# The last batch's output stages of a Mamba and SwiGLU block as a program of their own, with the last quad weighed in two parts

## The reference

```python
h  = x * rsqrt(mean(x*x) + 1e-5) * norm_w
xs, res = split(h @ in_proj_w.T)                  # 256 + 256 channels
u  = silu(conv4(xs) + conv_b)
delta, Bm, Cm = split(u @ x_proj_w.T, [64, 80])   # 64 + 16 + 16
delta = softplus(delta @ dt_proj_w.T + dt_proj_b)
state[t] = exp(delta * A) * state[t-1] + delta * u * Bm     # 256 channels x 16 states
y  = (sum over 16 states of state * Cm) + u * D
a  = (y * silu(res)) @ out_proj_w.T + x
x1 = layernorm(x + a)
out = layernorm(x1 + (silu(x1 @ wg.T) * (x1 @ wu.T)) @ wd.T)   # 384 hidden; weights are integers / 127
```

## Time and profile before

| | us |
|---|---|
| median of 3 runs | 580.98 |
| lowest, highest | 580.44, 583.85 |
| the profiled execution | 581.86 |
| its span, first to last instruction | 580.1 |

### The profile page before, as it was taken

One profiled execution on the slowest core, in us unless ns is written; L12 is line 12 of the kernel. 1 busy time (PEld: TensorE's weight loads), 2 busy tenths in 40 slices (PEclk: granted clock), 3 DMA queues, 4 the chain that ended last, 5 costly groups with the idle time before them and its releaser, 6 DMA issues.

```text
span 580.1 us, 6345 instructions
## 1 busy us (share of the span) xinstructions
PE 476.2 (82%) x1887; PEld 239.6 (41%) x1887; DVE 521.0 (90%) x562; ACT 367.2 (63%) x581; POOL 417.0 (72%) x214
## 2 busy tenths in 40 slices
PE   8988774989979996989978996989888996587574
PEld 6332431535542553534442553444443452243243
DVE  5869789998999899998999899999999899999924
ACT  3577865489458866589458866589458855544220
POOL 8758597857695796968695796868695796876010
PEclk9889976989979898989979897989979997769879
DMA  8063333600642032600551042501451042500000
GB/s 222 3 146 62 83 72 74 145 1 5 141 108 56 1 82 67 160 1 15 131 120 46 0 97 62 149 0 24 121 131 31 0 101 70 138 1 0 1 18 18
DMA packets 27368, 39.22 MB, mean 68 GB/s; under 512 B 3816, under 2 KB 10056, under 8 KB 27344
## 3 DMA queue, kind: packets, MB, share of 16 engines
q1 hardware_dynamic: 25424, 38.51, 27.9%
q10 hardware_dynamic: 1920, 0.42, 0.4%
HBM read 3.27 MB, written 2.10 MB: 9 GB/s over the span
## 4 chain that ended last, share of the span: by engine, by line
PE 27%; issue 23%; DVE 21%; POOL 18%; ACT 6%; DMA 2%; SPq 1%; POOLq 0%; DVEq 0%; ACTq 0%
DVE state L1038 14%; POOL prod L864 10%; PE dense_ps L464 6%; PE dense_ps L482 5%; PE y_ps L456 4%; DVE weighted L1046 3%; POOL z_wm L868 2%; ACT decay_ps L620 2%; POOL z_wm L870 2%; PE c_ps L442 1%; PE dense_ps L484 1%; PE dense_ps L506 1%; POOL z_wm L881 1%; PE dense_ps L502 1%; SPq L358 1%
## 5 line engine op out<-in xcount | busy, mean ns | idle before, releaser
L864 POOL TENSOR_TENSOR prod<-du_rep,b_rep 128x2048 f32<-128x2048 f32 x63 | 285.6, 4540 | 52.0 <-ACT b_rep L657 32.8
L1038 DVE TENSOR_TENSOR_SCAN state<-decay_ps,prod 128x512 f32<-128x512 f32 x256 | 299.1, 1207 | 19.5 <-ACT decay_ps L620 13.4
L620 ACT ACTIVATE decay_ps<-delta_rep,a_neg 128x512 f32<-128x512 f32 x252 | 170.6, 688 | 107.3 <-DVE state L1038 107.1
L1046 DVE TENSOR_TENSOR weighted<-state,c_ps 128x2048 f32<-128x2048 f32 x64 | 146.4, 2288 | 4.2 <-PE c_ps L442 2.3
L464 PE MATMUL dense_ps<-x_all,ident 128*128 128x256 f32 x348 | 102.5, 430 | 18.9 <-ACT bc L653 9.4
L464 PEld LDWEIGHTS dense_ps<-x_all,ident 128*128 128x128 f32 x348 | 67.1, 207 | 65.9 <-issue 21.2
L456 PE MATMUL y_ps<-weighted,gather 128*32 128x512 f32 x512 | 77.7, 683 | 17.0 <-DVE weighted L1046 17.0
L482 PE MATMUL dense_ps<-h_t,tap_t 128*128 128x512 f32 x128 | 58.5, 599 | 0.9 <-ACT h_t L668 0.9
L442 PE MATMUL c_ps<-bc,pick 64*128 64x512 f32 x64 | 34.7, 542 | 19.7 <-DVE weighted L1046 19.7
L442 PEld LDWEIGHTS c_ps<-bc,pick 64*128 64x128 f32 x64 | 12.8, 200 | 69.6 <-issue 38.5
L889 POOL TENSOR_TENSOR ve<-mv,epsm 128x4 f32<-128x4 f32 x14 | 2.8, 202 | 53.1 <-DVE mv L1057 53.1
(11 more groups left out here) (148 smaller groups left out, 628.6 us busy)
## 6 DMA issues: line engine op xcount, KB each, us to landing
du_rep<-z_wm SPq DMA_DIRECT2D x64, 256.0 KB, 4.7
delta_rep<-z_ln SPq DMA_DIRECT2D x64, 256.0 KB, 4.5
out_dram<-y_out SPq DMA_DIRECT2D x8, 256.0 KB, 2.2
state<-L_attn_in_proj_w_in ACTq DMA_DIRECT2D x1, 256.0 KB, 3.9
x_all<-L_attn_x_in SPq DMA_DIRECT2D x1, 256.0 KB, 4.3
weighted<-L_ffn_w_gate_in SPq DMA_DIRECT2D x1, 192.0 KB, 9.8
weighted<-L_ffn_w_up_in SPq DMA_DIRECT2D x1, 192.0 KB, 3.5
weighted<-L_ffn_w_down_in SPq DMA_DIRECT2D x1, 192.0 KB, 4.5
```

Source lines behind the costliest of these rows:

```text
L620: A(decay_ps[n % DECAYS][:, :], decay_ps[n % DECAYS][:, :] if spread_first else delta_rep[:, h, c, :], ACT.Exp, scale=a_neg[:, col:col + 1 ...
L864: TT(prod[quad % 2][:, :, :], du_rep[:, h, :, :], b, ALU.mult).then_inc(prod_ready, 1)
L1038: dve.tensor_tensor_scan(state[n // BLOCKS % 2][:, n % BLOCKS, :], decay_ps[n % DECAYS][:, :], prod[n // BLOCKS % 2][:, n % BLOCKS, :], 0. ...
L1046: TT(weighted[quad % 2][:, :, :], state[quad % 2][:, :, :], c_ps[:, :].unsqueeze(1).broadcast_to([P, BLOCKS, T]), ALU.mult).then_inc(weigh ...
```

## The change

Iteration 8 becomes a function `tail` of its own on PE, DVE and ACT, with semaphores of its own (`last_...`), and POOL's two powers are called there directly. In it:

- **The last quad is weighed in two parts.** In iteration 7, DVE weighs blocks 0 to 2 (1536 columns) before the last scan and block 3 (512 columns) after it. PE sums blocks 0 to 2 after the first part and block 3 after the second.
- **`proj` starts early.** Twice x and the part of g's half 0 are issued ahead of the last quad's sum; only the part of half 1 follows it.
- **Two half banks.** The 512 rows are split into two halves of two row blocks, in dense banks 0 and 1 (`half_ps`). Statistics start on a half when its bank is done. The scaling of half 0 is DVE's, that of half 1 ACT's (with a shift `nmr` = -mean * rs that DVE computes first); the transposes, and the copies to `x1_t`, are done by halves on the two engines.
- **All eight banks.** The six gate and up products go to six different banks (`rest_ps`), in the order gate0, up0, gate1, up1, gate2, up2, with no wait for a bank; `down(0)` stands ahead of up2. The x1 term of `down` is issued ahead of gate0.
- **Silu.** ACT applies Silu to the gate's bank, DVE multiplies with up in one instruction. The Silu table is asked for ahead of time by an activation of one column.
- **The store** is two transfers of 128 KB, SP's for half 0 and ACT's for half 1.

In the jobs of all batches, `proj` and `down` now go through their terms in the outer loop and the row blocks in the inner one, and wait for each term's input apart.

```diff
@@ PE: jobs of all batches
-                    it.wait(pe, g_ready, HALVES, -1, HALVES)
-                    for i in range(TILES):
-                        for h in range(HALVES):
+                    for h in range(HALVES):
+                        it.wait(pe, g_ready, HALVES, -1, h + 1)
+                        for i in range(TILES):
                             last = mm(ps[:, i * P:(i + 1) * P], g[:, h, i * P:(i + 1) * P], out_t[:, h, :],
...
-                    it.wait_taken(pe, f"up{HID - 1}")
-                    for i in range(TILES):
-                        for b in range(HID):
+                    for b in range(HID):
+                        it.wait_taken(pe, f"up{b}")
+                        for i in range(TILES):
@@ banks
+        half_ps = dense_ps[0:2]
+        rest_ps = decay_ps + dense_ps[2:] + [c_ps, y_ps]
@@ PE, iteration 8
+            def tail(it):
+                for b in range(DENSE):
+                    pe.wait_ge(taken[b], it.before[b])
+                pe.wait_ge(g_ready, HALVES * B - 1)
+                for half in range(2):
+                    for i, cols in half_tiles(half):
+                        mm(half_ps[half][:, cols], twice[:, :], x_all[:, (B - 1) * TILES + i, :],
+                           start=(cols.start == 0), stop=False)
+                        mm(half_ps[half][:, cols], g[:, 0, i * P:(i + 1) * P], out_t[:, 0, :], start=False, stop=False)
+                for c in range(BLOCKS):
+                    if c == 0:
+                        pe.wait_ge(last_weighed, 1)
+                    if c == BLOCKS - 1:
+                        pe.wait_ge(last_weighed, 2)
+                    last = mm(y_ps[DB * c:DB * c + DB, :], gather[:, :], weighted[(QUADS - 1) % 2][:, c, :],
+                              start=False, stop=True, tile_position=(0, DB * c))
+                last.then_inc(last_summed, 1)
+                pe.wait_ge(g_ready, HALVES * B)
+                for half in range(2):
+                    for i, cols in half_tiles(half):
+                        last = mm(half_ps[half][:, cols], g[:, 1, i * P:(i + 1) * P], out_t[:, 1, :],
+                                  start=False, stop=(i % HT == HT - 1))
+                    last.then_inc(last_full, 1)
...
+                for half in range(2):
+                    pe.wait_ge(last_x1[half], 1)
+                    for i, cols in half_tiles(half):
+                        last = turn(rest_ps[half][:, cols], x1[:, i, :], ident[:, :])
+                    last.then_inc(last_turned, 1)
+                for half in range(2):
+                    for i, cols in half_tiles(half):
+                        mm(half_ps[half][:, cols], ident[:, :], x1[:, i, :], start=(cols.start == 0), stop=False)
...
+                gate_or_up(gate_t, 0, 2, last_gate)
+                gate_or_up(up_t, 0, 3, last_up)
+                gate_or_up(gate_t, 1, 4, last_gate)
+                gate_or_up(up_t, 1, 5, last_up)
+                gate_or_up(gate_t, 2, 0, last_gate)
+                down(0)
+                gate_or_up(up_t, 2, 1, last_up)
+                down(1)
+                down(2)
@@ ACT, iteration 8 (after the second norm of batch 6)
+                A(a_exp[:, 0:1], cw[:, 0, 0:1], ACT.Silu)
...
+                norm_half(1, x1, rs1, nmr1).then_inc(last_x1[1], 1)
+                act.wait_ge(last_turned, 2)
+                A(x1_t[:, HC:], rest_ps[1][:, 0:HC], ACT.Copy).then_inc(last_xt[1], 1)
+                for b, bank in ((0, 2), (1, 4), (2, 0)):
+                    act.wait_ge(last_gate, b + 1)
+                    A(g_act[:, b, :], rest_ps[bank][:, :], ACT.Silu, scale=WSCALE).then_inc(last_silu, 1)
...
+                norm_half(2, y_out[it.next], rs2, nmr2).then_inc(last_y[1], 1)
+                act.wait_ge(last_y[1], 1)
+                act.dma_start(out.rearrange("b t m -> (b t) m")[B * T - HC:, :].rearrange("(i t) m -> t i m", t=P),
+                              y_out[it.next][:, HT:, :]).then_inc(last_out, 16)
@@ DVE, iterations 7 and 8
+                        if it.k0 == B - 1 and n == GROUPS - 2:
+                            weigh_last(it, 0, BLOCKS - 1)
+                        elif it.k0 == B - 1 and n == GROUPS - 1:
+                            weigh_last(it, BLOCKS - 1, BLOCKS)
...
+                def norm_rows(n, st, mv, ve, rs, nmr, dst, done):
+                    for half in range(2):
+                        dve.wait_ge(last_full, 2 * n - 1 + half)
+                        for i, cols in half_tiles(half):
+                            last = dve.bn_stats(st[:, i, :], half_ps[half][:, cols])
+                        last.then_inc(last_stats, 1)
...
+                    dve.wait_ge(last_rs, n)
+                    STT(out=nmr[:, HT:], in0=mv[:, HT:, 0], scalar=-1.0, in1=rs[:, HT:], op0=ALU.mult, op1=ALU.mult
+                        ).then_inc(last_nmr, 1)
+                    for i, cols in half_tiles(0):
+                        last = TS(dst[:, i, :], half_ps[0][:, cols], mv[:, i, 0:1], rs[:, i:i + 1],
+                                  ALU.subtract, ALU.mult)
+                    last.then_inc(done, 1)
...
+                for b, bank in ((0, 3), (1, 5), (2, 1)):
+                    dve.wait_ge(last_silu, b + 1)
+                    dve.wait_ge(last_up, b + 1)
+                    STT(out=g_act[:, b, :], in0=g_act[:, b, :], scalar=2.0 / WSCALE, in1=rest_ps[bank][:, :],
+                        op0=ALU.mult, op1=ALU.mult).then_inc(last_act, 1)
```

167 lines of the change are left out of this document (102 added, 65 removed).

## The result

| | before | after |
|---|---|---|
| median, us | 581.09 | **574.96** |
| lowest, highest | 580.44, 583.85 | 572.12, 575.79 |
| profiled execution | 581.86 | 575.49 |
| its span | 580.1 | 573.7 |

The medians differ by 6.1 us, 1.05%; the ratio estimated from the eight executions is 0.9876 (95% interval 0.9834 to 0.9918), 1.24% less. The forecast was 575.8 (573.8 to 578.4), worked out from a median before of 580.98; one more execution of before makes that 581.09.

A forecast was written before the change was run, and what follows sets the result against it. DVE was taken to bound the batches, and a chain with one engine working at a time the last 32.8 us. Tail terms gave 4.7 or 5.6 us by clock, middle 5.1, so median 575.8 us (range 573.8 to 578.4).

The forecast's parts named there:

- The batches: Scanned batches: the new loop orders of proj and down win 0, since DVE bounds the batch and waits for neither.
- The split weighing: Last quad's weighing: two parts add a fixed cost, so g starts 0.2 us later at the low clock.
- The hoisted products: Projection: 8 rows instead of 24 behind the sum, statistics end 1.6 us (low clock) or 2.6 (high) sooner.
- Statistics to gate0: First norm: 0.25 us won up to x1, then 0.25 won or 0.9 lost from x1 to gate0.
- Gate0 to down's end: Feed-forward part: 8.4 us at the high clock against 11.90, 3.5 us less.
- The end: Down's end to the span's end: 0.65 us won, by earlier statistics and shorter scaling; split stores taken as 0.
- second case: Tail with the high clock from the projection on: gate0 at 558.6, 5.6 us won in all.
- The first: Tail with the clock low until 561.3: gate0 at 560.5, 4.7 us won in all.
- Rival (a): Tail: TensorE's clock doesn't fall at all, 8.0 us won, 573.0 us; chance 0.1.
- Rival (b): Gate0 to down's end: the clock stays low through the feed-forward part, 584.0 us, slower than before; chance 0.03.
- (c): Tail: each of twelve chain steps costs 0.2 us more, 2.4 of the 5.1 lost, 578.3 us; chance 0.2.
- (d): Batches: PE's earlier finish in down reaches DVE, 2 us more won over seven, 573.8 us; chance 0.07.

The follow-up runs named there:

- e1: Kernel before with only the new loop orders of proj and down: median 581.44 us, ratio 1.0012.
- e12: e6 with fillers added ahead of the wait in PE's order of every batch, the old three kept: median 562.86 us, tail 29.2 us.
- e4: Changed kernel with nine 256-column filler products in PE's gap before the last sum: median 572.45 us, tail 29.35 us.
- e6: Changed kernel with one 2048-column weighing, nine fillers before the last sum and seven instead of two before the transposes: median 573.63 us, tail 29.19 us.
- e7: e6 with the hoisted proj products behind the last sum again and 13 fillers for 9: 573.74 us, tail 30.09 us.
- e9: e6 with the x1 term of down moved from ahead of gate0 to behind gate2: 574.35 us, tail 30.00 us.
- e8: e6 with Tanh and two DVE instructions per block instead of Silu and one, without the early table load: 573.39 us, tail 29.18 us.
- e2: Changed kernel with the old loop orders in proj and down for all batches but the last: median 574.98 us, tail 31.6 us.
- e3: Changed kernel with the last quad weighed in one 2048-column instruction after the last scan: median 574.25 us, tail 32.8 us.
- e5: Kernel before with more fillers, 12 instead of 1 ahead of the last sum and 8 instead of 2 ahead of the transposes: median 577.33 us, tail 34.27 us.
- e11: e6 with the three fillers ahead of z0 moved, one ahead of the C product and two behind the sum: median 573.26 us, tail 29.18 us.

## Why the prediction was right

The median came 0.8 us under the forecast, inside the forecast's own range. The most likely outcome had been a gain within 1% (chance 0.59, against 0.38 for more), and it came out just above. By its steps:

- *The batches, 0*: right for the change as far as e1 can tell. But the working took 2.8 us of DVE's idle time a batch as given. 1.4 to 2.0 of it is the clock's, as e12's batches show, and the step said nothing of that.
- *The split weighing, 0.2 later*: right. The last part ends 0.2 later than before (551.57, against 549.60 + 1.76), and at the high clock g comes 0.16 later (e4 against e6). In after g's start does not move, because the clock came back during the last block's sum (its last row took 0.88 us against 1.06).
- *The hoisted products, 1.6 or 2.6 at the end of the statistics*: 2.7 in the profile, where the clock was back for the projection, as the larger figure assumes. At equal clock the whole stage is worth 1.3, and the hoist alone 0.9 (e7): 1.4 of the 2.7, half, were the clock's work, which the text mixed with the program's.
- *Statistics to gate0, 0.25 and +0.25 or -0.9*: 0.7 won, 0.2 better than the high-clock figure. ACT's two blocks took 0.81 (costed at 0.87), and PE's x1 term hid the copies (e9: 0.8).
- *Gate0 to down's end at 8.4*: 8.21. The sum over PE's products was right, and Silu's share of it zero (e8), as costed.
- *The end, 0.65*: 1.05. Mis-sized term: the stores, taken as 0, won 0.30 (last issue to the end 2.33 against 2.63), with scaling 0.29 and the statistics' 0.45 beside it.
- *The Silu table, 0*: right. The load takes 1.28, the next activation starts 0.01 later and ACT waits 0.92 for DVE afterwards. The Trainium skill, page "ScalarE: Activation LUTs", section "What ACT_TABLE_LOAD costs", adds a drain of about 1.38 us; the trace doesn't show it, and the measurement decides.

Two sums of the working don't come out. Its parts for the high clock from the projection on, 2.6 + 0.25 + 0.25, make 3.1 at gate0 and not 2.9, so its second case should have been 5.8 instead of 5.6. And the headings "1.4 to 2.7" and "1.0 or 0.5" are not the figures that stand under them, 1.6 or 2.6 and +0.25 or -0.9.

The step that was wrong in kind is the clock's course. I let it be low until 561.3, which is 19.4 us into the tail; in the profile of after it was low from 5.9 to 9.3 us into it and then high to down's end. By the forecast's own sign ("I am wrong if the granted clock from 547 to 561 is not mostly low") this part failed, and with it sign (3): gate0 came 3.4 us sooner, not at most 3. With the measured course my own terms give 7.05 (2.9 to gate0, 3.5, 0.65), and the tail won 8.15. e2 (low at the sum and again at the gates, 6.6 won) is my second case in the same tail, forecast at 5.6, so that case does come. The first, forecast at 4.7, came only in e3 (13.7 us low, tail 5.4 won), which is another program in the tail. The forecasts of these two were 1.0 and 0.7 too small; the end is 0.4 of that in both, and the wrong sum 0.2 in e2.

So the closeness of the number is in part luck. In the profiled execution two misses of opposite sign met: the tail won 8.15 where the forecast had 5.1, and it started 1.76 us later where the forecast had 0. What the clock did in the tails of after's other three executions no trace shows; that the median averages over such courses, as e2's tail suggests, is an inference.

Rival (a), the clock never falls, is what e4 and e6 made by hand: 8.8 and 9.0 won in the tail, against its 8.0. Rival (b) didn't come. (c), fixed costs, is refuted: the small steps cost what their rows say. (d), 2 us more in the batches from the loop orders, is refuted by e1: its median is 0.6 above before's, and its interval reaches down to 0.6 us below and no further.

One thing is open: whether after's start at 543.71 is more than chance. Among the twelve kernels with the old quad order starts lie between 538.45 and 543.71 with no order by loop or tail. 1.6 of the 1.76 us are the second batch with its longer low stretch, but why the clock takes another course there in one execution and not in another is not shown; no run holds that course fixed and toggles only the change.

## What to carry to other kernels

Cut both traces at a shared event and compare what follows: the profiled execution's span moved 6.4 us, while the stage worked on moved 8.2 and its start moved back by 1.8, which no run ties to the change. Cost a shortened tail twice, at each level of TensorE's clock, and fill the gaps of both versions before judging what the program is worth. And when the bounding engine's batches come in two lengths, look at the clock in the longer one first: three more filler products a batch were worth 10 us, more than the whole rewritten tail.

## What the runs showed of the hardware

- The sum's eight rows, four blocks into 32 partitions each, take 1.07 us at the high clock (e5, e6) and 1.94 at the low one (before, e3), and a last block alone is no faster: from the end of the last weighing to g's start it is 1.13 us in e4 (one block left) and 1.19 in e6 (four). A shorter last block buys nothing.
- The busiest engine's batch follows the clock of another engine. A fall halfway of about 3 us makes it 1.4 us longer at equal clock in its first 5 us (e12's 63.4 against e3's 64.8): z's products come later, the decays behind them too, and DVE waits. Where the clock is low for about 7 or 10 us, the batch is 3.6 or 5.2 us longer than the shortest (66.4, 68.0 against 62.8), and DVE waits for C too.
- Fillers moved into one gap without adding any only move the fall: in e11 from 25 to 29 or 30 us into the batch, at 573.3 us. With three more kept behind the gap (e12) it doesn't fall there, at 562.9.
